# Local attention: row maxima applied as the bias of sixteen 64-column exponentials on ScalarE

## The reference, cut to what matters

```python
scores = jnp.einsum('bhqd,bhkd->bhqk', q, k) * scale          # 32 heads, scale = 64 ** -0.5
mask = (i[None, :] > i[:, None]) | (i[:, None] - i[None, :] >= WINDOW)   # WINDOW = 32
scores = jnp.where(mask[None, None], -jnp.inf, scores)
sink_col = jnp.broadcast_to(sinks[None, :, None, None], (Bq, H, Tq, 1))
combined = jnp.concatenate([scores, sink_col], axis=-1)
probs = jax.nn.softmax(combined, axis=-1)[..., :-1]
out = jnp.einsum('bhqk,bhkd->bhqd', probs, v)
```

## Time and profile before

| | us |
|---|---|
| median of 3 runs | 1837.38 (1836.09 to 1838.32) |
| the profiled execution, its own time | 1832.11 |
| its span in the profile | 1830.3 |
| a turn in the middle (start of `a0v`, 764.06, to the next, 941.53) | 177.5 |
| the two-sequence part, to about | 1475 |

### The profile page before, as it was taken

The page is one execution under the profiler, slowest core; times in us unless marked ns, Lnnn a source line. Parts: engine busy times, 40 slices in busy tenths (PEclk is TensorE's granted clock), DMA queues, the critical chain, the costliest instruction groups (busy, mean ns, idle before and its releaser), DMA issues.

```text
span 1830.3 us, 37451 instructions
## 1 busy us (share of the span) xinstructions
PE 1352.7 (74%) x14566; PEld 1024.7 (56%) x14566; DVE 1266.0 (69%) x2529; ACT 657.9 (36%) x1533; POOL 224.3 (12%) x375
## 2 busy tenths in 40 slices
...
DMA packets 51245, 70.82 MB, mean 39 GB/s; under 512 B 4912, under 2 KB 46576, under 8 KB 49520
## 3 DMA queue, kind: packets, MB, share of 16 engines
...
## 4 chain that ended last, share of the span: by engine, by line
issue 66%; PE 15%; DVE 8%; POOL 4%; ACT 3%; DMA 2%; POOLq 0%; SPq 0%; DVEq 0%; ACTq 0%
PE ps L900 11%; POOL rstd L1337 3%; POOL rstd L1336 1%; DMA out<-ptf 1%; PE ps L904 1%; DVE experts L675 1%; PE ps L472 1%; ACT big L1256 1%; PE ps L1002 1%; DMA ptf<-in_spread 1%; PE ps L398 1%; DVE ptf L1509 1%; ACT experts L517 0%; PE ps L445 0%; DMA kf<-in_dn 0%
## 5 line engine op out<-in xcount | busy, mean ns | idle before, releaser
L1256 ACT ACTIVATE big<-ps,st 128x128 f32<-128x128 f32 x768 | 205.6, 407 | 205.6 <-DVE st L1590 205.6
L1002 PE MATMUL ps<-ident,big 128*128 128x128 f32 x1024 | 183.7, 347 | 34.6 <-ACT big L1256 18.3
L1509 DVE TENSOR_TENSOR ptf<-ps,ptf 128x1024 f16<-128x1024 f32 x128 | 154.4, 1221 | 64.7 <-ACT ptf L1262 63.4
L1002 PEld LDWEIGHTS ps<-ident,big 128*128 128x128 f32 x1024 | 163.0, 185 | 61.4 <-ACT big L1256 31.7
L1336 POOL TENSOR_TENSOR rstd<-mv,eps 128x1 f32<-128x1 f32 x80 | 18.4, 229 | 1274.4 <-DVE mv L1400 1274.4
L1262 ACT ACTIVATE ptf<-ps 128x1024 f16<-128x1024 f32 x128 | 130.6, 1031 | 88.9 <-PE ps L1002 88.8
L1588 DVE TENSOR_REDUCE st<-ps 128x8 f32<-128x1024 f32 x96 | 117.0, 1218 | 35.5 <-PE ps L900 35.5
L900 PE MATMUL ps<-wo,qhl 128*128 128x256 f32 x512 | 119.6, 388 | 15.4 <-DVE qhl L1514 13.2
L900 PEld LDWEIGHTS ps<-wo,qhl 128*128 128x128 f32 x512 | 96.0, 192 | 32.9 <-issue 15.2
L900 PE MATMUL ps<-experts,ptf 128*128 x312 | 100.4, 383 | 0.0
L1242 ACT ACTIVATE qhl<-big 128x1024 f16<-128x1024 f32 x32 | 33.8, 1057 | 162.9 <-DVE big L1474 160.6
...
## 6 DMA issues: line engine op xcount, KB each, us to landing
...
```

The source lines that it names most:

```text
L1002: m = pe.transpose(ps_f(u, j // 4, P, (j % 4) * P), big[u][:, j * P:(j + 1) * P], ident[:])
L1256: m = f(big[u][:, c], ps_all[u][:, c], ACT.Exp, scale=scale, bias=st32[u][:, 3, j:j + 1])
L1509: S(u, tt(pt_l[u][:, c], ps_all[u][:, c], pt_h[u][:, c], ALU.subtract), f"pt{n}l{h}")
```

## The change

In `shifted0` the subtraction of 128x1024 on DVE goes. Instead DVE multiplies the 16 maxima by minus the scale into row 3 of `st32`. In `exps` ACT's one exponential of 1024 columns becomes sixteen of 64 columns that read the scores in PSUM, each with its head's column of `st32` as bias. All four tables are new: the cycle of stages begins at another place (so the loop's branch lies elsewhere on each engine), and within the cycle stages have moved.

```diff
@@ exps
                     f(st32[u][:, 1, k], st32[u][:, 1, k], ACT.Exp, scale=scale)
-                    c = slice(1024 * h, 1024 * h + 1024)
-                    m = f(big[u][:, c], big[u][:, c], ACT.Exp, scale=scale)
+                    for j in range(16 * h, 16 * h + 16):
+                        c = slice(j * 64, j * 64 + 64)
+                        m = f(big[u][:, c], ps_all[u][:, c], ACT.Exp, scale=scale, bias=st32[u][:, 3, j:j + 1])
@@ shifted0
-                b16 = big[u][:, c].rearrange("p (a t) -> p a t", a=16)
...
                 mark(tt(st32[u][:, 1, k], sinkT[:, k], m_, ALU.subtract))
-                S(u, tt(b16, p16, m_[:, :, None].to_broadcast([P, 16, 64]), ALU.subtract), f"s0m{h}")
+                S(u, ts(st32[u][:, 3, k], m_, -SCALE0, None, ALU.mult), f"s0m{h}")
@@ VECTOR_TURN, first line
-0:a0v 1:q1 0:k0 1:q2 1:q3 1:q4 1:ql0 1:ql1 0:v0 0:k0l 0:q1 1:s00 0:q2 0:q3 0:q4 0:ql0 0:ql1 1:s01 1:n00 1:n01
+0:l11 0:a11 1:pk3v 0:a12 1:mv 0:a13 1:s3a0 0:n2 1:s3a1 0:xT2 0:a15v 0:a15t 1:l3a0 0:a16v 1:l3a1 0:a17v 1:a22a
```

More of the change, by code:

```diff
@@ L90 @@
 TENSOR_TURN = """
[L91 to L95, removed]
@@ L96 @@
-0:mx1 0:mx2 1+a22 0+a0 1+a23 0+a1a 0+a1b 0+a1c 0+a20 0+a21 1+a3m 1+a30 1+a31 0+a22 0+a23 1+a32 1+a33 0+a3m
-0+a30 0+a31 0+a32 0+a33 1+T00 1+T01 1+a50 1+a51 1+a52 1+a53 1+a60
+1:c3b0 0:tr3 1:c3b1 0:a19 1:T3b0 1:T3b1 0:pk3 1:pv3b 1:pv3bz 0:memp 0:c3a0 1:tr4 0:c3a1 1:mx1 1:mx2 0:T3a0
+0:T3a1 1+a0 0:pv3a 0:pv3az 0:c3b0 0:c3b1 1+a1a 1+a1b 0:T3b0 0:T3b1 1+a1c 0:pv3b 0:pv3bz 1+a20 1+a21 0:tr4
+0:mx1 0:mx2 1+a22 0+a0 1+a23 0+a1a 0+a1b 0+a1c 1+a3m 1+a30 1+a31 1+a32 1+a33 0+a20 0+a21 0+a22 1+T00 0+a23
+1+T01 1+a50 1+a51 1+a52 1+a53 1+a60 0+a3m 0+a30 0+a31 0+a32 0+a33 1+a61 0+T00 1+kv1 0+T01 0+a50 1+tr1 0+a51
@@ L102 @@
[L102 to L103 removed]
+1:h10 1:h11 0:kvm 0:rk 0:rq 1:a15s 0:qT1 0:e10 0:e11 0:h10 1:a19s 0:h11 1:qT3 1:e3a0 1:e3a1 0:a15s 1:h3a0
+1:h3a1 1:e3b0 1:e3b1 0:a19s 1:h3b0 1:h3b1 0:qT3 1:a31s 0:e3a0 0:e3a1 0:h3a0 0:h3a1 1+a0s 0:e3b0 0:e3b1 0:h3b0
+0:h3b1 1+v0h 1+k0h 0:a31s 0+a0s 1+qh0 1+qh1 0+v0h 0+k0h 1+e00 1+e01 1+h00 1+h01 1+o0a 1+o0c 0+qh0 0+qh1 0+e00
@@ L104 @@
+0+e01 0+h00 1+kvm 1+rk 0+h01 0+o0a 1+rq 1+qT1 0+o0c 1+e10 1+e11
 """
 POOL_TURN = """
-1:pq 0:rs1 0:pk 1:rs2 0:pq 1:rs3 0:rs2 0:rs3 1:rs4 1+rs0 0:rs4 0+rs0 1+rs1 1+pk
+0:pk 1:rs2 0:pq 1:rs3 0:rs2 0:rs3 1:rs4 1+rs0 0:rs4 0+rs0 1+rs1 1+pk 1+pq 0+rs1
 """
 VECTOR_TURN = """
-0:a0v 1:q1 0:k0 1:q2 1:q3 1:q4 1:ql0 1:ql1 0:v0 0:k0l 0:q1 1:s00 0:q2 0:q3 0:q4 0:ql0 0:ql1 1:s01 1:n00 1:n01
-1:l00 1:l01 0:s00 1:o0b 1:o0d 0:s01 0:n00 0:n01 1:a6v 1:kvv 1:n1 1:kvp 1:xT1 0:l00 0:l01 1:a7k 1:a7v 1:a8
-1:a7q 0:o0b 0:o0d 1:s10 1:s11 0:a6v 1:l10 1:l11 0:kvv 0:n1 0:kvp 1:a11 0:xT1 1:a12 0:a7k 1:a13 0:a7v 1:n2 0:a8
```

15 lines of the change are left out of this document (9 added, 6 removed).

## The result

The changed kernel takes 1880.72 us (median of four runs, 1877.34 to 1887.00), the kernel before 1837.07 us (1836.09 to 1838.32). The ratio is 1.0241, with a 95% interval of 1.0213 to 1.0269: 43.6 us slower, where 11 were forecast and 28.6 was the upper end of the range. The profiled execution took 1877.34 us; its span is 1875.5 us, 45.2 more than that of before. One later execution, of the kernel with DVE's list begun at `s10` and `a6v` left where the change has it, took 2151 us at a mean granted clock of 0.55, where its four others took 1860 to 1867; it is left out of every comparison.

What follows compares the result with a forecast made beforehand. DVE limits only the local attention stretch, chains between engines the rest. Turn terms of +1.6 us and branch +9.3 give +10.9 us: 1843.0 us for the profiled execution, 1848.3 us as median; range 1822 to 1866.

Steps and rivals of the forecast that it cites:

- The exponentials: Local attention: sixteen 64-column exponentials on ACT at 0.213 us each, start to start; row sums wait 2.2 and 0.65 us.
- Rival D: Attention stretch: exponentials dearer than the fit, 0.267 us each giving 1876 us, or 0.240 us giving 1862; chance 0.10.
- The relief is nearly all given back.: Attention stretch: 4.2 us less DVE work a turn is nearly offset by new waits, net -0.4 us a turn.
- `l10` and `l11` ahead of `a6v`: DVE order: `a6v` of sequence 0 stands behind these two operations and its statistics come late, +1.1 us a turn.
- DVE's branch: Loop branch between `a19e` and `l11`: 2.8 us exposed, 1.25 us won at `a0v`, +1.55 us net six times, +9.3 us.
- Rival C: Loop branch ahead of `l11`: DVE's branch is hidden, the rest as summed, 1831.5 us, 0.3% faster; chance 0.22.
- the branch as a whole: Loop branch at its new places: DVE's costs +1.55 us net six times, ACT's is taken as nothing.
- rival B: PE pause before `T00` of sequence 1: half clock through projection `a60`, +2.5 us a turn on top, 1868 us; chance 0.12.

## Why the direction was right and the size wrong

- **The exponentials.** Right: 0.211 us each against 0.213, waits of 1.70 to 1.94 and 0.41 us against 2.2 and 0.65. Rival D, dearer ones (0.240 or 0.267 us), is out. But 1.94 us at `n00` of sequence 0 is not in every turn: it is 0.66 in the fourth. And the scores of sequence 0, for which 1.0 us of waiting was forecast, are waited for 2.79 us in the fifth turn, 1.04 and 1.18 us in the fourth.
- **"The relief is nearly all given back."** Forecast were -0.4 us a turn. At full clock it is mis-sized: counted from `a0v`, the fourth turn is 1.6 us early at `s00` of sequence 0 and 2.5 to 2.7 us early at `s10` of sequence 1 (65.15 us against 67.6 to 67.9 before). At half clock all of it is gone (68.2 to 70.6 us; all from the second turn on). Whether it pays also depends on the order: in the old one 1.0 us a turn stays. The prediction costed arithmetic and order together, and so did not see that they pull against each other.
- **`l10` and `l11` ahead of `a6v`.** Right: 1.03 us a turn in every turn, forecast 1.1.
- **DVE's branch.** Right in place and size: 2.5 to 2.8 us bare ahead of `l11`, six times, 15.6 in all, and 1.25 us won at `a0v`; 9.3 us forecast, 11.1 when undone. Rival C, that it is hidden, is out.
- **The step that failed first: the branch as a whole.** The prediction asked for DVE's and ACT's branch and did not ask for PE's, which the same rotation of the lists moved from behind `a60`, where it shows 0.18 us, to `c3b0`. There it shows 3.0 to 3.2 us, and `xT3` of sequence 0 starts 1.9 us later for it, some 11 us in six turns. Moving it back did not win these 11 us: the time stayed (1870.57 us) or fell by 3.7, as the half clock came more often; at equal clock a turn was 2.5 to 3.1 us shorter. With it, a turn at full clock comes out: 1.75 us forecast with the branch, and 1.9, against 3.56 measured (181.02 against 177.47). This agreement is partly luck. At `n2` of sequence 0, behind DVE's branch, the delay is 1.3 us where the terms give 3.0 (mostly the 2.1 to 2.3 us by which the attention stretch is better than forecast), and behind `xT3` another 1.4 us appear by `l3b0`, which waits 2.87 us for ACT (1.95 before). The terms ahead of the branch and behind it were off in opposite directions.
- **The step that failed most: TensorE's clock, which the sum puts at nothing and leaves to rival B with a chance of 0.12.** Rival B had the place and the price right, half clock in the new `a60` and 2.5 us a turn, and the cause wrong: it blames the pause ahead of `T00` of sequence 1, and where that pause is long `a60` is mostly at full. Measured: in five turns of seven 1.8 to 5.7 us more than in one of 181.0, 17 us in all, 2.5 us on average. It was held unlikely since "sequence 0's queries, dense matmuls, lie between". They did lie between, and the clock fell behind them. The row that might have warned is in the earlier trace rows: after PE's pause the clock stood at 0.60 on average for 17 us, and dense transposes and products were among them. In the orders of before that stretch ends just ahead of `a60` (1.00 from 804 us on in the trace); the new order shifted the two against each other.

The forecast of 1848.3, with 11 us for PE's branch and 17 for the clock, is 1876 us. Measured were 1880.7 us. That these sums meet is not a proof: at full clock the attention stretch is over 2 us a turn better than forecast, and the 1.4 us behind `xT3` have no term. What makes the clock fall where it does stays open.
